# A fused memory-attention and FFN kernel: maxima across partitions by TensorE, q1 converted as it lands, the first g and h on GpSimd, q2 loaded ahead of the next x

## The reference

```python
# attention: a memory M (128 x 128) that is updated at each of 2048 positions
q, k, v = xn @ Wq.T, xn @ Wk.T, xn @ Wv.T
r_t = q_t @ M.T;  M = 0.99 * M + v_t.T @ k_t / b      # over t
s = (r @ Wo.T) * sigmoid(gate)
# FFN with quantised weights, groups of 128 rows share a scale
h  = layernorm(xn) * gamma + beta
w1 = (fc1_q - 128) * fc1_scales                       # 512 x 2048, int32 input
y  = silu(h @ w1 + b1)
w2 = (fc2_q - 128) * fc2_scales                       # 2048 x 512, int32 input
z  = y @ w2 + b2
out = x + s * silu(xn + 0.5 * z)
```

## Time and profile before

| | |
|---|---|
| median of 3 runs | 1309.07 us (1308.35 to 1309.46) |
| profiled execution | 1311.27 us, its span 1309.4 us |
| PE busy | 1197.3 us, 91% |
| VectorE (DVE) busy | 1139.7 us, 87% |
| ScalarE (ACT) busy | 894.6 us, 68% |
| GpSimd (POOL) busy | 801.2 us, 61% |
| granted TensorE clock, mean | 0.973 of full speed |
| HBM read, written | 47.59 MB, 16.81 MB |

### The profile page before, as it was taken

The page is one execution under the profiler, slowest core; times in us unless marked ns, Lnnn a source line. Parts: engine busy times, 40 slices in busy tenths (PEclk is TensorE's granted clock), DMA queues, the critical chain, the costliest instruction groups (busy, mean ns, idle before and its releaser), DMA issues.

```text
span 1309.4 us, 18606 instructions
## 1 busy us (share of the span) xinstructions
PE 1197.3 (91%) x5888; PEld 605.9 (46%) x5888; DVE 1139.7 (87%) x1964; ACT 894.6 (68%) x1549; POOL 801.2 (61%) x758
## 2 busy tenths in 40 slices
PE   1249899999999999999999999999999999999993
PEld 1015445454555555454554545455455545455540
DVE  6758898989899898989899898989989898988986
ACT  0526677767777767777687776778776777767771
POOL 4137774756838484775947475683848477494623
PEclk9669999999999999999999999999999999999997
DMA  9700112030302103040211203021210304020111
GB/s 273 244 11 1 33 38 61 4 95 1 79 19 55 43 19 79 1 98 1 65 33 38 60 1 97 1 74 24 52 46 17 81 2 97 1 65 1 37 30 32
DMA packets 41620, 65.68 MB, mean 50 GB/s; under 512 B 11696, under 2 KB 11952, under 8 KB 41008
## 3 DMA queue, kind: packets, MB, share of 16 engines
q1 hardware_dynamic: 41232, 64.36, 18.9%
q10 hardware_dynamic: 288, 0.08, 0.0%
HBM read 47.59 MB, written 16.81 MB: 49 GB/s over the span
## 4 chain that ended last, share of the span: by engine, by line
PE 77%; DVE 11%; issue 6%; ACT 3%; POOL 2%; DMA 1%; SPq 0%; ACTq 0%; POOLq 0%; DVEq 0%
PE blk L455 29%; PE blk L473 28%; PE side L416 9%; DVE blk L678 4%; PE side L440 4%; PE side L432 2%; DVE y_split L669 2%; PE side L399 1%; DVE y_split L664 1%; PE side L433 1%; PE side L434 1%; PE side L425 1%; DVE g_lo L648 1%; DMA xt<-in_x 1%; ACT h_full L520 1%
## 5 line engine op out<-in xcount | busy, mean ns | idle before, releaser
L678 DVE TENSOR_TENSOR blk<-blk,ratio_rows 128x512 f32<-128x512 f32 x960 | 642.1, 687 | 90.4 <-PE blk L473 86.8
L558 ACT ACTIVATE blk<-blk,ratio 128x512 f32<-128x512 f32 x768 | 507.7, 665 | 236.3 <-PE blk L455 225.8
L455 PE MATMUL blk<-h_split,q_sb 128*128 128x512 f16 x2048 | 613.3, 381 | 35.7 <-ACT q_sb L591 29.0
L473 PE MATMUL blk<-w_sb,y_split 128*128 128x512 f16 x2048 | 610.4, 380 | 1.2 <-DVE blk L678 1.2
L473 PEld LDWEIGHTS blk<-w_sb,y_split 128*128 128x128 f16 x2048 | 200.0, 98 | 247.2 <-DVE blk L678 6.8
L455 PEld LDWEIGHTS blk<-h_split,q_sb 128*128 128x128 f16 x2048 | 196.3, 98 | 250.8 <-issue 63.2
L565 ACT ACTIVATE y_full<-blk,par,last 128x512 f32<-128x512 f32 x256 | 201.1, 785 | 109.7 <-PE blk L455 109.4
L669 DVE SCALAR_TENSOR_TENSOR y_split<-y_full,up,y_split 128x512 f16<-128x512 f32 x256 | 217.1, 848 | 0.1
L956 POOL CAST h_split<-h_full 128x512 f16<-128x512 f32 x60 | 50.4, 840 | 250.5 <-ACT h_full L520 250.5
L664 DVE TENSOR_SCALAR y_split<-y_full,up 128x512 f16<-128x512 f32 x256 | 158.2, 618 | 0.0
L948 POOL TENSOR_SCALAR g_rows<-xt,mv,gs 128x512 f32<-128x512 f32 x60 | 133.1, 2225 | 0.0
(11 more groups left out here) (132 smaller groups left out, 1016.3 us busy)
## 6 DMA issues: line engine op xcount, KB each, us to landing
xt<-in_x SPq DMA_DIRECT2D x64, 256.0 KB, 4.8
x_again<-in_x SPq DMA_DIRECT2D x256, 64.0 KB, 1.9
out<-z_rows SPq DMA_DIRECT2D x256, 64.0 KB, 1.7
w_sb<-in_q SPq DMA_DIRECT2D x4, 1024.0 KB, 14.2
ratio_rows<-ratio_dram SPq DMA_DIRECT2D x4, 1024.0 KB, 15.7
y_split<-in_q SPq DMA_DIRECT2D x1, 1024.0 KB, 10.5
h_split<-in_q SPq DMA_DIRECT2D x1, 1024.0 KB, 12.7
z_rows<-in_q SPq DMA_DIRECT2D x1, 1024.0 KB, 14.3
```

The costliest lines, as they stand in the source:

```text
L455: mm = pe.matmul(blk[J % 2][:], q1_sb[:, g, j // 4, w, j % 4 * P:(j % 4 + 1) * P], a[:, c % 2, g, :], start=(g == 0 and n == 0), stop=(g = ...
L473: mm = pe.matmul(blk2[:, i, :], y[:, J % Y_RING, rows], w2_sb[:, j, part, :], start=(j == 0 and n == 0), stop=(j == FB - 1 and n == len(te ...
L558: act.activation(blk[J % 2][:], blk[J % 2][:], ACT.Copy, scale=ratio1[:, at:at + 1]).then_inc(blk_scaled, 1)
L678: dve.tensor_tensor(blk2[:, i, :], blk2[:, i, :], ratio2_rows[:, j, :], ALU.mult).then_inc(blk2_scaled, 1)
```

## The change

What it does, part by part:
- The four maxima over the partitions (parameters, wqkv, q1, q2) no longer use partition_all_reduce. VectorE writes maxima per partition into a 32-column tile `tops`; PE transposes it, VectorE reduces it to one column and multiplies it with a 32x32 identity (`pick`), PE multiplies a matrix of ones with that diagonal, so that every partition has all values, and VectorE reads them (`largest`). The parameters' maxima come first, wqkv's has a round of its own.
- q1 is converted by ScalarE alone: the first eight of 16 pieces in the setup part as their quarters land, with factor 1.0 and shift -128 (if the maximum turns out above 1920, all are made again); the other eight in slots 3, 6, ..., 24. The factor's bound is at least TOP (2^14), so that it is 1.0 unless values are large. The clearing of the low parts moves from GpSimd to ScalarE.
- The first g (four `normalise`) and both parts of the first h are made by GpSimd, the transposes of the first g go row tile by row tile as g is made, and ScalarE makes h_full before g_hi.
- SyncE issues q2 directly behind b2, then waits for the first g and issues x(1), and only then waits for ratio2_made. fc2's ratios are made by VectorE in slot 2.
- In the first chunk the maxima of q2 are at slots 0, 1, 5 and 9, its factor at 12 and 13, its 16 conversions from slot 14 (before: 10); statistics of x(1) at 18, 20, 22, 24, moments at 26 and 27, rows(1) at 28 (before: 0 to 6, and 7). Later chunks are as before.

The diff, cut to its core (declarations and the branches for large q1 are left out):

```diff
-PREPARE_AT, ROWS_AT = (0, 3, 15, 18), 7
+FIRST_STATS_AT, FIRST_MOMENTS_AT = (18, 20, 22, 24), (26, 27)
+PREPARE_AT, ROWS_AT, FIRST_ROWS_AT = (0, 3, 15, 18), 7, 28
-TOP_Q2_AT, Q2_SCALE_AT = (0, 1, 2, 3), 9
-Q2_AT = tuple(10 + 3 * n for n in range(FB))
+Q1_AT = tuple(3 + 3 * n for n in range(FB // 2))
+RATIO2_AT, TOP_Q2_AT, Q2_SCALE_AT = 2, (0, 1, 5, 9), 12
+Q2_AT = tuple(14 + 3 * n for n in range(FB))
...
 # SyncE, behind the load of b2_half
-            sp.wait_ge(ratio2_made, 1)
-            sp.dma_start(ratio2_dram.rearrange("j (p n) -> p j n", n=KC), ratio2[:].rearrange("p (j n) -> p j n", n=KC)).then_inc(ratio2_stored, 16)
             for n in range(4):
                 sp.dma_start(q2_in_sb[:, 4 * n:4 * n + 4, :], q2.rearrange("(n j p) h -> n p j h", n=4, p=P)[n]
                              ).then_inc(q2_in[n], 16)
+            g_wait(sp, 0)
+            load_x(1)
+
+            sp.wait_ge(ratio2_made, 1)
+            sp.dma_start(ratio2_dram.rearrange("j (p n) -> p j n", n=KC), ratio2[:].rearrange("p (j n) -> p j n", n=KC)).then_inc(ratio2_stored, 16)
             sp.wait_ge(ratio2_stored, 16)
...
 # PE
+            def turn_tops(n):
+                pe.wait_ge(tops_made, n + 1)
+                pe.transpose(top_bank[n][0:32, 0:P], tops[:, n % 2, :], ident[:]).then_inc(tops_turned, 1)
+            def spread_tops(n):
+                pe.wait_ge(diag_made, n + 1)
+                pe.matmul(top_bank[n][:, P:P + 32], ones[:], top_diag[:], start=True, stop=True
+                          ).then_inc(tops_spread, 1)
...
+                    if G == Q2_SCALE_AT:
+                        turn_tops(OF_Q2)
+                    if G == Q2_SCALE_AT + 1:
+                        spread_tops(OF_Q2)
...
-            for k in range(KC):
-                turn(0, k, first_turn_bank[k])
+            for n in (OF_PARAMS, OF_WQKV):
+                turn_tops(n)
+                spread_tops(n)
+            for i in range(NT):
+                pe.wait_ge(g_done, i + 1)
+                for k in range(KC):
+                    mm = pe.transpose(first_turn_bank[k][:, i * P:(i + 1) * P], g_rows[:, i, k * P:(k + 1) * P],
+                                      ident[:])
+                    if i == NT - 1:
+                        mm.then_inc(turn_done, 1)
+            turn_tops(OF_Q1)
+            spread_tops(OF_Q1)
...
 # ScalarE
+            act.activation(q1_sb[:].rearrange("p g q t n -> p (g q) t n")[:, :, 1, :],
+                           zero_c[:].unsqueeze(1).to_broadcast([P, FB, T]), ACT.Copy).then_inc(q1_low_zero, 1)
...
-            for k in range(KC):
-                g_high(0, k, first_turn_bank[k])
-                h_whole(0, k, first_turn_bank[k])
-            act.activation(wqkv_hi[:], wqkv_in, ACT.Copy, scale=up_wqkv).then_inc(wqkv_hi_done, 1)
+            def q1_piece(n, scale, shift):
+                g, quarter = n % 4, n // 4
+                act.wait_ge(q1_in[quarter], 16)
+                act.activation(q1_sb[:, g, quarter, 0, :], q1_in_sb[quarter][:, g, :], ACT.Identity,
+                               bias=shift, scale=scale).then_inc(q1_done, 1)
...
+            for n in range(FB // 2):
+                q1_piece(n, 1.0, minus_point[:, 0:1])
+            act.wait_ge(wqkv_scale, 1)
+            act.activation(wqkv_hi[:], wqkv_in, ACT.Copy, scale=up_wqkv).then_inc(wqkv_hi_done, 1)
+            for k in range(KC):
+                h_whole(0, k, first_turn_bank[k])
+                g_high(0, k, first_turn_bank[k])
...
+                if G in Q1_AT:
+                    if G == Q1_AT[0]:
+                        act.wait_ge(q1_ready, 1)
+                    q1_piece(FB // 2 + Q1_AT.index(G), up_q1, q1_shift[:, 0:1])
...
 # VectorE
+            def pick(n):
+                dve.wait_ge(tops_turned, n + 1)
+                link(dve.tensor_reduce(top_col[:, n:n + 1], top_bank[n][0:32, 0:P], AX.X, ALU.max))
+                dve.tensor_scalar(top_diag[:], ident[0:32, 0:32], top_col[:, n:n + 1], None, ALU.mult
+                                  ).then_inc(diag_made, 1)
+            def largest(n, to):
+                dve.wait_ge(tops_spread, n + 1)
+                link(dve.tensor_reduce(to, top_bank[n][:, P:P + 4], AX.X, ALU.max))
...
+            top(OF_WQKV, 0, wqkv_in, AX.XY).then_inc(tops_made, 1)
+            top_of_q1(0)
+            pick(OF_WQKV)
+            largest(OF_WQKV, top_wqkv[:])
+            link(dve.tensor_scalar(bound[:, 1:2], top_wqkv[:], TINY, None, ALU.max))
+            link(dve.tensor_scalar(pow2[:, 1:2].bitcast(I32), bound[:, 1:2].bitcast(I32), 0x7F800000, None,
+                                   ALU.bitwise_and))
+            link(dve.reciprocal(up_wqkv, pow2[:, 1:2]))
+            dve.tensor_scalar(up_wqkv, up_wqkv, TOP, None, ALU.mult).then_inc(wqkv_scale, 1)
+            top_of_q1(1)
...
+            top_of_q1(2)
+            g_low(0, 0, first_turn_bank[0])
+            top_of_q1(3).then_inc(tops_made, 1)
+            g_low(0, 1, first_turn_bank[1])
+            pick(OF_Q1)
+            dve.wait_ge(wqkv_hi_done, 1)
+            dve.scalar_tensor_tensor(wqkv_lo[:].rearrange("p k n -> p (k n)"),
...
+            largest(OF_Q1, top_q1[:])
...
+            g_low(0, 2, first_turn_bank[2])
+            g_low(0, 3, first_turn_bank[3])
...
+                if G == RATIO2_AT:
+                    hold(1, s2_c, KC, FB)
+                    ratios(1, ratio2, KC)
...
+                if G == Q2_SCALE_AT:
+                    pick(OF_Q2)
+                if G == Q2_SCALE_AT + 1:
+                    largest(OF_Q2, top_q2[:])
                     q2_scale()
...
 # GpSimd
             rows(0)
-            pool.wait_ge(tops_done, 1)
-            pool.partition_all_reduce(all_tops[:], tops[:], P, bass.bass_isa.ReduceOp.max).then_inc(all_tops_done, 1)
-
-            pool.memset(q1_sb[:, :, :, 1, :], 0.0).then_inc(q1_low_zero, 1)
...
+            for i in range(NT):
+                normalise(0, i)
             row_scales(0)
...
+            for k in range(KC):
+                h_high(0, k)
+                h_low(0, k)
             pool.wait_ge(b2_in, 16)
```

More of the change, by code:

```diff
@@ L513, in g_high @@
                 wait(act, qkv_done, 4 * c)
-                act.activation(g_hi[:, k, :], bank[:], ACT.Copy)
+                made = act.activation(g_hi[:, k, :], bank[:], ACT.Copy)
+                if c == 0:
+                    made.then_inc(first_g_hi_done, 1)
             def h_whole(c, k, bank):
-                if c == 0 and k == 0:
+                if c == 0:
                     act.wait_ge(h_scales, 1)
+                    act.wait_ge(turn_done, k + 1)
                 wait(act, h_done, 4 * c + k - 1)
@@ L596, in _ @@
             with act.If(slow > 0):
[L597 to L599 removed]
+                q1_again()
             act.wait_ge(wo_in, 16)
@@ L946, in normalise @@
                     pool.wait_ge(rows_done, c + 1)
-                    pool.wait_ge(turn_done, 4 * c)
+                    wait(pool, turn_done, 4 * c)
                 pool.tensor_scalar(g_rows[:, i, :], xt[:, i, :], mv[:, c % 2, i, 0:1],
@@ L952, in h_high @@
                 pool.wait_ge(h_full_done, 4 * c + k + 1)
+                if k == 0 and c == 1:
+                    pool.wait_ge(q1_done, FB // 2)
+                    pool.wait_ge(q1_ready, 1)
                 if k == 0 and c >= 2:
@@ L1019, in _ @@
                                pattern=[[-1, P]], channel_multiplier=1).then_inc(ident_done, 2)
+            pool.memset(ones[:], 1.0).then_inc(ones_done, 1)
             for at, value in ((EPS_AT, EPS), (MINUS_HALF, -0.5), (HALF, 0.5), (G_SCALE_AT, G_SCALE),
@@ L1062, in _ @@
                     output(*at)
-                if c < NCH - 1 and e == ROWS_AT:
+                if c < NCH - 1 and e == (ROWS_AT if c else FIRST_ROWS_AT):
                     rows(c + 1)
```

227 lines of the change are left out of this document (95 added, 132 removed).

## The result

| | before | changed |
|---|---|---|
| median of the runs, us | 1309.26 | 1291.03 |
| lowest to highest, us | 1308.35 to 1311.23 | 1290.21 to 1294.66 |
| profiled execution, us (span) | 1311.27 (1309.4) | 1291.07 (1289.2) |
| granted clock over the span | 0.973 | 0.986 |
| first fc1 / first fc2 / qkv of slot 65, us | 52.38 / 94.31 / 158.70 | 36.10 / 65.30 / 137.82 |

A forecast was written before the change was run, and what follows sets the result against it. Loop bound by TensorE, so all gain lies in 103 us of front and first-chunk excess. Terms: 33.3 + 2 - 1.5 - 3 = 30.8 us off span 1309.4, adjusted to the median: 1278.3 us, range 1268 to 1291.

The forecast's parts named there:

- rows(1): GpSimd's rows(1), moved to slot 28 between two q2 conversions: PE stops at slot 35's read, +3 us (0 to 6).
- first fc1: End of the front: PE begins fc1 at 38.5 us instead of 52.4, with q1_scale near 37.3.
- first fc2: Slot 16: first fc2 product at 61 us instead of 94.31, a gain of 33.3 us.
- slots 16 to 65: First chunk after first fc2: -2 us clock, +1.5 us statistics and moments of x(1), +3 us rows(1).
- rival 3: Quicker front: small DVE instructions don't wait (2 us), rows(1) absorbed (3), normalises' stop shrinks (3); 1270, chance 0.16.
- q2_scaled: Slots 12 and 13: q2's factor ready at 58.5 us, after the pick and q2_scale, nine small instructions.
- rival 2: Ratios late before slot 16: their store to DRAM needs its 12.9 us again; 1285, chance 0.1.
- a clock already up: From slot 16: PE is fairly busy before it, so the clock may be up already, -2 us.
- rival 1: Conversions: DVE and GpSimd in lockstep, rows(1) fully on PE (5.7 us), clock drop 2 us; 1287, chance 0.2.
- The meeting of the h splits with the last conversions: End of the first chunk, in rival 1: chunk 1's h splits meet four conversions instead of two; no separate size.
- The stop by the normalises: Between q2 conversions: PE's 3.19 us wait at 135.76 mostly stays; rival 3 has it shrink (3 us).
- ScalarE's share of the front: Setup: zero fill, eight q1 pieces and wqkv_hi on ACT, free between 22 and 28: hidden, at worst 1 us.

The follow-up runs named there:

- The probe: Changed kernel plus a memset and six tiny VectorE instructions on a spare tile, run while GpSimd makes g; its one execution took 1290.4 us.
- the early pick: Changed kernel with VectorE's pick of q2's maxima in slot 12 moved ahead of its wait for r_t; 1291.59 us, ratio 0.9851.

## Why the prediction was right, and where its sizes were wrong

The direction and the place were right: all the gain lies before slot 65, and the loop is untouched. The size was not: 18.2 us instead of 30.8, and 1291.03 us lies at the very end of the range (1268 to 1291), 12.7 us above the forecast. Of these, 4.3 us are the first fc2, 5.6 us slots 16 to 65 (8.1 against 2.5), 0.7 us the rest, and 2.1 us no mechanism: the forecast took 2.2 us off because the profiled execution of before was that much slower than its median, and for the changed kernel the two are equal. By steps:

- **First fc1** forecast 38.5, measured 36.10. The small DVE instructions were to wait beside g, with wqkv_scale at 24.4; it was there at 19.1. The rule cited from the Trainium skill ("SBUF — State Buffer", § Who interferes with whom) has conditions there that the prediction left out: a DVE instruction with at most one SBUF input, outside the two-port modes, doesn't contend with GpSimd. The one-column instructions beside g (0.15 to 0.17 us) and the waits beside the cast and the tensor_tensor of GpSimd agree with that. The probe's tensor_tensor with two SBUF inputs doesn't: it took 0.52 us where the page has it wait for the end; the measurement decides. The quick small instructions are a part of rival 3 that came true. A round over PE took 1.46 us (16.89 to 18.35) from the pick to the end of the read back, against the 1.3 assumed; PE's transpose, 0.40 us at 14.84, ran beside a reduction and is not in it.
- **q2_scaled** forecast 58.5, measured 58.1. But DVE had been 3 us ahead, and gave it back in the wait for r_t (54.77): I had counted DVE's instructions in slots 0 to 16 and not its waits.
- **First fc2** forecast 61, measured 65.30: the failed step. I took it as q2_scaled plus the three steps of one conversion (2.5 us). Two things stood in the way. The q2_high was behind y_high of J=2, which waited for fc1 products behind a half-clocked qkv group; and behind that lay PE's branch at slot 16, which no term of the sum held at all. In the changed kernel the first alone decides; the run with the early pick removed it and met the second, and the run without the branch showed what that was. The kernel before branches at the same place, and its trace had the row, which I read past:

```profile
93.51 1.01 PE L455 MATMUL blk<-h_split,q_sb 128*128 128x512 f16 x2 [1.50 <-issue]
```

  1.50 us without a releaser, with the flag written at 75.2.
- **Ratios late** (rival 2) did not happen: the store took 5.1 us (45.89 to 50.98), as taken, the quickest of the four 1 MB loads of the rows landed 4.6 us after its issue (6 were assumed, from no row), and VectorE never waited for a row. The transfer has a price all the same, through what it slows: 2.5 us at the branch, in the kernel with the early pick.
- **Slots 16 to 65**: -2 us for a clock already up did come, as the rows at 65.30 and 94.31 show. The second step that failed is rows(1), taken at 3 us (0 to 6): with the statistics, taken at 1.5, it cost 6 to 7 us. The place was right, the read of slot 35. I had let PE absorb four slots of it; PE ran on for 2.5 us after VectorE had stopped at 86.2, and then stood for 5.5 us, with half clock behind. This is rival 1's mechanism, whose price of 5.7 plus 2 us was near the right one (the rows give 5.73, not 5.75). The meeting of the h splits with the last conversions, also named there, cost 2.03 and 1.32 us and 2 us of half clock, where the kernel before had a single stop:

```profile
152.69 0.66 PE L399 MATMUL side<-ident,g_rows 128*128 128x128 f32 x4 [1.52 <-DVE g_lo L648]
```

  The stops at 70.28 and 75.77 (2.1 us) are new and stood in no term. The stop by the normalises shrank from 3.19 to 1.22 us (113.15), as rival 3 has it. In all PE is idle for 12.4 us in this stretch instead of 5.3 and busy for 60.1 instead of 59.1. The forecast of 128 for slot 65 stands against 137.82.
- **ScalarE's share of the front** was to be hidden, and is: it is free at 20.7, and g waits for GpSimd. For the same reason the early half of q1 brought nothing that can be seen.

What happened is rival 1's mechanism and a late first fc2. That rival 1's 1287 and the 4.3 us of the first fc2 make 1291 is luck in part: early stops, the chunk's end, the smaller stop by the normalises and the 2.1 us of the median happen to balance. The terms of slots 16 to 65 were each taken near the middle of their bounds, as if they were independent, while one cause, DVE and GpSimd in lockstep with PE behind them, bore on all of them.

## What to carry to other kernels

A step moved between two engines in lockstep can cost its full length, and the clock that the stop takes with it: put it where the receiving engine has nothing due, as rows(1) in slot 13 (6 us here). Ask of each wait in a hand-ordered program what is queued behind it, and look for branches on the path: their price shows as idle time with no releaser, and here it was higher beside heavy DMA (5.88 us against 3.39). When a stop is gone, look for the next one before adding gains up: one early pick was worth nothing alone.

## What the runs showed of the hardware

- PE's way through a data-dependent branch: 4.6 us from the flag's write to the first matmul with almost no DMA traffic, 7.1 us beside traffic of 406 to 438 GB/s, PE being idle for the last 3.39 and 5.88 us of it. Why 4.6 us, where 1.50 us stood with the flag long known, stays open.
- The gap on GpSimd behind an all-reduce of 0.39 us: 7.36 us alone, 12.21 us with the ratio rows' transfer beside it.
- Beside GpSimd's 2.07-us tensor_scalar with two per-partition operands, DVE's tensor_scalar of 1 or 2 columns takes 0.15 to 0.29 us. Beside its memset of 6.99 us one of 2 columns takes 6.60 us, beside its tensor_tensor of 1.15 us one of 16 columns 1.21 us, and beside its cast of 0.60 us a tensor_tensor of one column 0.58 us.
